# A latent-attention layer with a block-quantised FFN: the weight quantisation moved into the weight-transpose stage, and four tile buffers for the two x sweeps

## The chip, the cores and the metric

The kernel runs on the 8 cores of one Trainium2 chip. Each core works alone on its part, without collectives: core pairs share one of the four batch rows, and each core of a pair owns every other block of 128 tokens. The metric is device time in microseconds (us) of the slowest core. The time before is 4926.94 us, the median of 2 runs (4926.56 to 4927.32).

## The reference

```python
xn = _layernorm(x, axis=-1)                       # x: (4, 4096, 1024) f32
x = x + attn(xn, Wq, Wkv, Wk, Wv, Wo, q_g, k_g) + ffn(xn, weight, bias)

def attn(x, ...):                                 # 16 heads of 64
    q  = rms_norm((x @ Wq) per head, q_g)         # only the first 32 of 64 are used in scores
    kv = x @ Wkv                                  # 128 latent columns
    k  = rms_norm((kv @ Wk) per head, k_g)        # 32 per head
    v  = (kv @ Wv) per head                       # 32 per head
    probs = softmax(causal(q[..., :32] @ k.T / 8))
    return pad(probs @ v) @ Wo

def ffn(x, weight, bias):                         # blocks of 32 along the row
    def quant(t): s = max(max|block| / 7.5, 1e-30); return nearest_on_fp6_grid(block / s) * s
    return quant(x) @ quant(weight).T + bias
```

## The kernel before

Every engine runs one hand-written program. The same Python walk is emitted once for each engine, and `Walk._emit` turns each operation's list of tokens into semaphore waits on the engine that runs it; DMAs are issued by SyncE ("sync") in program order, so a DMA that waits holds every DMA behind it. A transpose (`pet`, L156) and most matmuls (`mm`, L151) wait for `w.tok("dv")`, which is the last VectorE operation emitted so far. All DMA issues have the line L144, and the waits before them L108.

The stages follow each other:

- **Statistics** (`stats`, L387 on). 32 tiles of 128 tokens of x are loaded, alternating between the two halves of `o_tm` (`tmt(0)`, `tmt(1)`). VectorE forms the row sum (L395), the square into `qs(3)` (L397) and its row sum (L400). A tile buffer is free when L400 is done. `stat_finish` turns the sums into mean and reciprocal deviation.
- **kv** (L481 to L517). The 32 tiles are loaded again into the same two buffers. Each is transposed in eight pieces, with a copy out of PSUM after each (L504), and multiplied by Wkv; the buffer is free after the last product (L512).
- **q** (L591 to L664). The same over the 16 tiles of the core's own tokens: row vectors of mean and deviation (L597, L601, L605), eight transposes and copies (L612), 144 matmuls with Wq (L630 reads them out), the norm (L634 to L657). After tiles 0, 2, 4 ... 14 the function `wd_quant` is called for one of eight tiles of the FFN weight: SyncE loads 128 rows of `dfw` into `xet(0)` or `xet(1)` (the two halves of `o_probs`), VectorE quantises them with `quant` (L332 to L385, 25 operations, result in `qtm()`), and SyncE stores the result to a scratch tensor `dwdq` in DRAM.
- **Weight transposes** (L675 to L689). The eight tiles of `dwdq` are loaded into `tmt`, transposed in eight pieces, and copied to `wdT` (L686).
- **FFN** (to L797). `qtile` loads a tile of x, quantises it (`quant` with mean and deviation, from L329), transposes it and copies it (L756); `ffn_half` multiplies by `wdT`.
- **Attention** in four passes over 1024 keys each, and then **normalisation and output** (L1007 to L1074).

The weight quantisation's order around a q tile is

```python
t_qz = quant(w, o_probs + 1024 * bi2, None, None,
             [t_lw] + ([wdq_st[wt - 1]] if wt else []))
wdq_st[wt] = dma("sync", dwdq[128 * wt:128 * wt + 128, :], qtm()[:], waits=[t_qz])
```

Of the kernel before, what the change touches and what calls it, by code (L numbers as in the profile page):

```python
# [5 lines left out]
F32 = mybir.dt.float32  # L6
OP = mybir.AluOpType
AF = mybir.ActivationFunctionType
AX = mybir.AxisListType.X
# [83 lines left out]
class Walk:  # L93
# [44 lines left out]
    def dma(self, q, out, in_, waits=()):  # L138
        pool = DMA_POOL[q]
        sem = pool[self.rr[q] % len(pool)]  # L140
        self.rr[q] += 1
        prior = self.cnt[sem]
        flow = [(sem, prior)] if prior > 0 else []
        return self._emit(q, lambda e: e.dma_start(out=out, in_=in_), sem, 16,  # L144
                          list(waits) + flow)
# [13 lines left out]
    def dve(self, fn, waits=()):  # L159
        return self._emit("vector", fn, "dv", 1, waits)  # L160
# [6 lines left out]
def build_nc(T=4096, stop_after=None):  # L167
# [6 lines left out]
    NO = OWN // 128  # L174

    nc = bass.Bass("TRN2", target_bir_lowering=False)
    dx = nc.dram_tensor("xb", [T, 1024], F32, kind="ExternalInput").ap()
# [8 lines left out]
    dfw = nc.dram_tensor("fw", [1024, 1024], F32, kind="ExternalInput").ap()  # L186
# [7 lines left out]
    dpn = nc.dram_tensor("patnorm", [8, 16, 128], F32, kind="ExternalInput").ap()  # L194
    ddeni = nc.dram_tensor("denind", [1, 528], F32, kind="ExternalInput").ap()
    dout = nc.dram_tensor("out", [1024, OWN], F32, kind="ExternalOutput").ap()
    dwdq = nc.dram_tensor("wdq", [1024, 1024], F32, kind="Internal").ap()

    from contextlib import ExitStack
    es = ExitStack()  # L200
    with es:
# [17 lines left out]
        o_probs = alloc(2 * 1024)  # L219
# [13 lines left out]
        o_tm = alloc(2 * 1024)  # L233
# [26 lines left out]
        idt = lambda: tl(o_id, 128)  # L260
        rowp = lambda p0, off, w: tl(o_rows + off, w, p0, 1)
        stc = lambda k, c, w=1: tl(o_stat + k * 32 + c, w)
# [4 lines left out]
        tmt = lambda i: tl(o_tm + i * 1024, 1024)  # L267
        qs = lambda i, off=0, w=1024, p0=0, p=128: tl(o_qs + i * 1024 + off, w, p0, p)
        qsc = lambda i: tl(o_qsc + i * 32, 32)
        qtm = lambda: tl(o_qtm, 1024)  # L270
# [9 lines left out]
        xet = lambda i: tl(o_probs + 1024 * i, 1024)  # L280
# [106 lines left out]

        def stats(w, dsrc, ntiles, tuse):
            dve, dma = w.dve, w.dma
            last = None  # L390
            for it in range(ntiles):
                bi = it % 2
                t_l = dma("sync", tmt(bi)[:], dsrc[128 * it:128 * it + 128, :],
                          waits=[tuse[bi]])
                t1 = dve(lambda e, it=it, bi=bi: e.reduce_sum(  # L395
                    stc(0, it), tmt(bi)[:], AX), waits=[t_l])
                t2 = dve(lambda e, bi=bi: e.tensor_tensor(qs(3), tmt(bi)[:],  # L397
                                                          tmt(bi)[:], OP.mult),
                         waits=[t1])
                last = dve(lambda e, it=it: e.tensor_reduce(  # L400
                    stc(1, it), qs(3), AX, OP.add), waits=[t2])
                tuse[bi] = last
            return last

        def stat_finish(w, n, t_in):
# [16 lines left out]
        def emit(w: Walk):  # L422
            dve, act, mm, pet, dma = w.dve, w.act, w.mm, w.pet, w.dma
# [17 lines left out]
            for i in range(8):  # L441
# [9 lines left out]
                waits=[t_eps])  # L451
# [8 lines left out]
                    waits=[t])  # L460
            for rr in range(4):
# [3 lines left out]
                     waits=[t, t_o16])  # L465
# [5 lines left out]
            for i in range(8):  # L471
# [3 lines left out]
                         waits=[tmm])  # L475

            tuse = [None, None]
            t_st = stats(w, dx, NT, tuse)
            t_fin = stat_finish(w, NT, t_st)

            tuse = [t_fin, t_fin]  # L481
            t_kv_prev = None
            for it in range(NT):
                bi = it % 2
                t_l = dma("sync", tmt(bi)[:], dx[128 * it:128 * it + 128, :],
                          waits=[tuse[bi]])
                tpm = pet(bank(3, 0, 128, 0, 1), stc(0, it), idt(),
                          waits=[t_fin, w.tok("dv")])
                t_evm = dve(lambda e: e.tensor_copy(mrow(), bank(3, 0, 128, 0, 1)),
                            waits=[tpm])  # L490
                tpa = pet(bank(6, 0, 128, 0, 1), stc(3, it), idt(),
                          waits=[t_fin, w.tok("dv")])
                t_eva = dve(lambda e: e.tensor_copy(arow(), bank(6, 0, 128, 0, 1)),
                            waits=[tpa])
                tra = mm(bank(7, 0, 128), onesr(128), arow(), True, True,
                         waits=[t_eva, t_or])
                t_ar = dve(lambda e: e.tensor_copy(areps(), bank(7, 0, 128)),
                           waits=[tra])
                t_ev = []
                for ci in range(8):  # L500
                    tp = pet(bank(ci // 4, 128 * (ci % 4), 128),
                             tmt(bi)[:, 128 * ci:128 * ci + 128], idt(),
                             waits=[t_l, w.tok("dv")])
                    t_ev.append(dve(lambda e, ci=ci: e.tensor_copy(  # L504
                        xfms(ci), bank(ci // 4, 128 * (ci % 4), 128)), waits=[tp]))
                for ci in range(8):
                    tmm = mm(bank(2, 0, 128), wkvt(ci), xfms(ci), ci == 0, False,
                             waits=[t_ev[ci]] + ([t_kv_prev] if ci == 0 else []),
                             inc=False)
                tmm = mm(bank(2, 0, 128), cskv(), mrow(), False, True,  # L510
                         waits=[t_evm, t_cskv])
                t_kv = dve(lambda e, it=it: e.tensor_tensor(  # L512
                    kvf(128, 128 * it), bank(2, 0, 128),
                    areps()[0:LAT, :], OP.mult), waits=[tmm, t_ar])
                t_kv_prev = t_kv
                tuse[bi] = t_kv
            t_kv_done = w.tok("dv")  # L517

            if stop_after == "A":
                tA = dma("sync", dout[0:LAT, 0:min(OWN, T)], kvf(min(OWN, T), 0),  # L520
                         waits=[t_kv_done])
# [3 lines left out]
            t_wq = []  # L525
            for i in range(8):
                t_wq.append(dma("sync", wqt(i), dwq[128 * i:128 * i + 128, :],
                                waits=[t_kv_done]))
            tuse = [t_kv_done, t_kv_done]
            tg1 = pet(bank(4, 0, 128, 0, NT), stc(2, 0, NT), idt(),  # L530
                      waits=[t_fin, w.tok("dv")])
            tg1e = dve(lambda e: e.tensor_copy(tl(o_scr2, 128, 0, NT),
                                               bank(4, 0, 128, 0, NT)),
                       waits=[tg1])
            tg2 = pet(bank(5, 0, 128, 0, NT), stc(3, 0, NT), idt(),
                      waits=[t_fin, w.tok("dv")])
            tg2e = dve(lambda e: e.tensor_copy(tl(o_scr2 + 128, 128, 0, NT),
                                               bank(5, 0, 128, 0, NT)),
                       waits=[tg2])
            g1 = mm(bank(4, 128, 128, 0, NO), oselt(), tl(o_scr2, 128, 0, NT),  # L540
                    True, True, waits=[tg1e, t_osel])
            g2 = mm(bank(5, 128, 128, 0, NO), oselt(),
                    tl(o_scr2 + 128, 128, 0, NT), True, True,
                    waits=[tg2e, t_osel])
            e1 = dve(lambda e: e.tensor_copy(tl(o_scr2, 128, 0, NO),
                                             bank(4, 128, 128, 0, NO)),
                     waits=[g1])
            e2 = dve(lambda e: e.tensor_copy(tl(o_scr2 + 128, 128, 0, NO),
                                             bank(5, 128, 128, 0, NO)),
                     waits=[g2])  # L550
# [5 lines left out]
                     waits=[b1])  # L556
            f2 = dve(lambda e: e.tensor_copy(stc(3, 0, NO), bank(5, 256, NO)),
                     waits=[b2])
            t_fin = dve(lambda e: e.tensor_scalar(stc(0, 0, NO), stc(2, 0, NO),
                                                  -1.0, None, OP.mult),  # L560
                        waits=[f1, f2])
            t_csq = None
            for ch in range(2):
                for i in range(8):
# [3 lines left out]
                             inc=i == 7)  # L568
                t_csq = dve(lambda e, ch=ch: e.tensor_copy(
                    csq(512 * ch, 512), bank(7, 0, 512, 0, 1)), waits=[tmm])  # L570
            t_pe0 = w.tok("pe")
            wdq_st = [None] * 8
            t_wdq_use = [None, None]

            def wd_quant(wt):
                bi2 = wt % 2
                t_lw = dma("sync", xet(bi2)[:],
                           dfw[128 * wt:128 * wt + 128, :],
                           waits=[t_pe0, t_kv_done] +
                                 ([t_wdq_use[bi2]] if t_wdq_use[bi2] else []))  # L580
                t_qz = quant(w, o_probs + 1024 * bi2, None, None,
                             [t_lw] + ([wdq_st[wt - 1]] if wt else []))
                wdq_st[wt] = dma("sync", dwdq[128 * wt:128 * wt + 128, :],
                                 qtm()[:], waits=[t_qz])
                t_wdq_use[bi2] = t_qz

            t_prev_q = [None] * 8
            t_prev_rep = None
            t_prev_lnq = None
# [1 line left out]
            for ot in range(NO):  # L591
                bi = ot % 2
                t_l = dma("sync", tmt(bi)[:], dxo[128 * ot:128 * ot + 128, :],
                          waits=[tuse[bi]])
# [64 lines left out]
                        scr2(256, 128), OP.mult), waits=[t_rp])  # L659
                    t_prev_rep = t_32  # L660
                tuse[bi] = t_32
                for wt in range(8):
                    if wt * NO // 8 == ot:
                        wd_quant(wt)  # L664
            t_q32_done = w.tok("dv")

            if stop_after == "B":
# [7 lines left out]
            t_wdT = None  # L675
            for wt in range(8):
                bi = wt % 2
                t_l = dma("sync", tmt(bi)[:], dwdq[128 * wt:128 * wt + 128, :],
                          waits=[tuse[bi], wdq_st[wt], t_wq[wt]])
                tp_last = None  # L680
                for ci in range(8):
                    tp = pet(bank(ci // 4, 128 * (ci % 4), 128),
                             tmt(bi)[:, 128 * ci:128 * ci + 128], idt(),
                             waits=[t_l, w.tok("dv")])
                    tp_last = tp
                    t_wdT = dve(lambda e, ci=ci, wt=wt: e.tensor_copy(  # L686
                        wdT(ci)[:, 128 * wt:128 * wt + 128],
                        bank(ci // 4, 128 * (ci % 4), 128)), waits=[tp])
                tuse[bi] = tp_last  # L689
            if stop_after == "C0":  # L690
                for ci in range(4):
                    dma("sync", dout[128 * ci:128 * ci + 128, 0:min(OWN, 1024)],
# [438 lines left out]
```

How the kernel before makes its waits and increments, by code:

```python
    def wait(self, engname, tok):  # L103
        if tok is None or self.cur != engname:
            return
        sem, val = tok
        if val > self.waited[sem]:
            self.h.wait_ge(self.sems[sem], val)
            self.waited[sem] = val
# [16 lines left out]
    def _emit(self, engname, fn, inc, amt, waits):  # L126
        for t in waits:
            self.wait(engname, t)
        if self.cur == engname:
            inst = fn(self.h)
            if inc is not None and inst is not None:
                inst.then_inc(self.sems[inc], amt)
        if inc is not None:
            self.cnt[inc] += amt
            return (inc, self.cnt[inc])
        return None
```

## Time and profile before

| | us |
|---|---|
| median of 2 runs | 4926.94 |
| the profiled execution | 4966.13 |
| span of its slowest core (core 3) | 4964.5 |
| spans of all cores | 4917.7 to 4964.5 |
| TensorE (PE) busy | 3414.2 (69%) |
| VectorE (DVE) busy | 1221.0 (25%) |
| ScalarE (ACT) busy | 627.3 (13%) |

The profile is one execution, read on its slowest core. Busy shares are averages over stages that differ: the page's slices show VectorE at 7 tenths in the first and around 1600 to 2000 us, and TensorE near 9 tenths only in attention. "PE" is a matmul or transpose, "PEld" the load of its stationary operand, "SPq" SyncE's queue, and the granted clock (PEclk) is the share of full speed that TensorE was given, so 0.50 is 1.2 GHz and 1.00 is 2.4 GHz. A wait "A <- B" is idle time of A that ended when B was done.

### The profile page before, as it was taken

Reading aid. Unit: us, or ns where it says so; the run is one execution under the profiler, and the core shown is the slowest. Engines: PE = TensorE matmul, PEld = TensorE weight load, DVE = VectorE, ACT = ScalarE, POOL = GpSimd, SP = SyncE. Lnnn points to the kernel's source line nnn. Section 1 sums busy time; section 2 is a strip of 40 time slices with the busy share of each in tenths; the row PEclk is TensorE's granted clock in tenths of the full one; section 3 lists DMA queues with packets and bytes.
Section 4 is the critical chain, followed back from the end, with each engine's and each line's share of the span. In section 5 each row is a group of like instructions: output and inputs, shape, how many; then the busy total and the mean of one; then the engine's idle time right before and its main releaser. Section 6 shows DMA issues by size and latency. Waiting matters only on the chain.

```text
span 4964.5 us, 61945 instructions; the slowest of 8 cores (4917.7 to 4964.5 us)
## 1 busy us (share of the span) xinstructions
PE 3414.2 (69%) x26106; PEld 2629.1 (53%) x26106; DVE 1221.0 (25%) x2264; ACT 627.3 (13%) x587; POOL 85.2 (2%) x164
## 2 busy tenths in 40 slices
PE   0455555555554146547899999799987997955787
PEld 0233334444443012212588888388874883755777
DVE  7322223333333666671100000200001002022000
ACT  0000000000000000000133433034330331210000
POOL 0000000000000000000000000000000000001111
PEclk6555566766666567768699999699986997866787
DMA  3111010000000100000000000000000000000221
GB/s 121 59 34 39 30 60 17 17 17 17 18 17 26 34 13 30 34 17 26 1 2 2 2 2 2 0 2 2 2 1 1 2 2 1 18 22 22 61 64 56
DMA packets 53208, 110.38 MB, mean 22 GB/s; under 512 B 8838, under 2 KB 27078, under 8 KB 52936
## 3 DMA queue, kind: packets, MB, share of 16 engines
q1 hardware_dynamic: 47816, 97.89, 6.1%
q0 software_dynamic: 5120, 8.53, 0.7%
q8 instruction: 211, 3.46, 0.3%
q14 instruction: 61, 0.50, 0.0%
HBM read 85.29 MB, written 20.97 MB: 21 GB/s over the span
## 4 chain that ended last, share of the span: by engine, by line
PE 61%; DVE 20%; issue 7%; ACT 7%; DMA 4%; SPq 1%; DVEq 1%; POOL 0%; ACTq 0%; POOLq 0%
PE psA L151 35%; PE psB L151 20%; ACT arena L935 6%; PE psA L156 5%; DMA arena<-xown 2%; DVE arena L504 1%; SPq L144 1%; DVE arena L397 1%; DVE arena L395 1%; DVE arena L756 1%; DVEq L108 1%; DVE arena L612 1%; DVE arena L400 1%; DMA arena<-arena 1%; DVE arena L879 1%
## 5 line engine op out<-in xcount | busy, mean ns | idle before, releaser
L151 PE MATMUL psA<-arena 32*128 32x128 f32 (+5 forms) x15616 | 2081.5, 316 | 336.2 <-DVE arena L1007 103.3
L151 PEld LDWEIGHTS psA<-arena 32*128 32x128 f32 (+4 forms) x15616 | 1783.1, 210 | 640.4 <-issue 608.9
L151 PE MATMUL psB<-arena 128*64 128x128 f32 (+3 forms) x9814 | 1078.7, 327 | 241.8 <-ACT arena L935 74.5
L151 PEld LDWEIGHTS psB<-arena 128*64 128x64 f32 (+3 forms) x9814 | 741.2, 155 | 547.9 <-issue 528.7
L935 ACT ACTIVATE arena<-psA,arena 128x1024 f32<-128x1024 f32 x544 | 604.2, 1115 | 1334.5 <-PE psA L151 1334.5
L156 PE MATMUL psA<-arena 128*128 128x128 f32 (+1 forms) x608 | 263.2, 433 | 729.4 <-DVE arena L385 255.4
L156 PEld LDWEIGHTS psA<-arena 128*128 128x128 f32 (+1 forms) x608 | 106.5, 175 | 886.6 <-issue 886.6
L967 DVE TENSOR_TENSOR arena<-psB,arena 128x1024 f32<-128x1024 f32 x24 | 29.4, 1225 | 936.6 <-PE psB L151 936.6
L156 PE MATMUL psB<-arena 128*1 128x128 f32 (+2 forms) x68 | 22.2, 329 | 238.2 <-DVE arena L385 202.4
L642 ACT ACTIVATE arena<-psB,arena 16x128 f32<-16x128 f32 x16 | 5.8, 360 | 1411.4 <-PE psB L151 1411.4
L963 DVE COPY arena<-psB 128x1024 f32<-128x1024 f32 x16 | 19.6, 1225 | 653.9 <-PE psB L151 653.9
L156 PEld LDWEIGHTS psB<-arena 128*1 128x1 f32 (+2 forms) x68 | 5.5, 83 | 255.6 <-issue 255.6
L1074 DVE TENSOR_TENSOR arena<-psA,arena 128x128 f32<-128x128 f32 x128 | 28.4, 283 | 379.0 <-PE psA L151 378.8
L504 DVE COPY arena<-psA 128x128 f32<-128x128 f32 x256 | 74.7, 292 | 181.3 <-PE psA L156 181.3
L841 ACT ACTIVATE arena<-psA,arena 16x1024 f32<-16x1024 f32 x4 | 4.4, 1107 | 859.8 <-PE psA L151 859.8
L630 DVE TENSOR_TENSOR arena<-psA,arena 128x128 f32<-128x128 f32 x128 | 28.3, 284 | 327.8 <-PE psA L151 327.8
L144 POOL DMA_DIRECT2D arena<-arena x32 | 16.6, 524 | 4527.9 <-DVE arena L967 4389.3
L144 POOL DMA_DIRECT2D arena<-out x128 | 68.4, 535 | 322.4 <-DVE arena L1074 302.5
L879 DVE COPY arena<-psA 128x512 f32<-128x512 f32 x64 | 27.7, 433 | 181.3 <-PE psA L151 181.3
L612 DVE COPY arena<-psA 128x128 f32<-128x128 f32 x128 | 37.3, 292 | 106.0 <-PE psA L156 106.0
L756 DVE COPY arena<-psA 128x128 f32<-128x128 f32 x128 | 37.3, 292 | 102.2 <-PE psA L156 102.2
L655 DVE COPY arena<-psB 128x128 f32<-128x128 f32 x64 | 18.7, 292 | 125.1 <-PE psB L151 125.1
(84 smaller groups left out, 937.4 us busy)
## 6 DMA issues: line engine op xcount, KB each, us to landing
arena<-xb SPq DMA_DIRECT2D x64, 512.0 KB, 3.5
arena<-xown SPq DMA_DIRECT2D x48, 512.0 KB, 4.4
out<-arena SPq DMA_DIRECT2D x32, 256.0 KB, 2.1
arena<-out POOLq DMA_DIRECT2D x128, 64.0 KB, 2.5
out<-arena SPq DMA_DIRECT2D x128, 64.0 KB, 2.0
arena<-wq SPq DMA_DIRECT2D x8, 512.0 KB, 9.5
arena<-fw SPq DMA_DIRECT2D x8, 512.0 KB, 5.7
wdq<-arena SPq DMA_DIRECT2D x8, 512.0 KB, 3.0
```

Of the source, the lines that this page charges most:

```text
L108: self.h.wait_ge(self.sems[sem], val)
L144: return self._emit(q, lambda e: e.dma_start(out=out, in_=in_), sem, 16, list(waits) + flow)
L151: lambda e: e.matmul(out, lhsT, rhs, start=start, stop=stop, tile_position=tp, skip_group_check=skipg),
L156: return self._emit("tensor", lambda e: e.transpose(out, in_, ident), "pe", 1, waits)
L395: t1 = dve(lambda e, it=it, bi=bi: e.reduce_sum(stc(0, it), tmt(bi)[:], AX), waits=[t_l])
L397: t2 = dve(lambda e, bi=bi: e.tensor_tensor(qs(3), tmt(bi)[:], tmt(bi)[:], OP.mult), waits=[t1])
L400: last = dve(lambda e, it=it: e.tensor_reduce(stc(1, it), qs(3), AX, OP.add), waits=[t2])
L504: t_ev.append(dve(lambda e, ci=ci: e.tensor_copy(xfms(ci), bank(ci // 4, 128 * (ci % 4), 128)), waits=[tp]))
L612: t_ev.append(dve(lambda e, ci=ci: e.tensor_copy(xfms(ci), bank(ci // 4, 128 * (ci % 4), 128)), waits=[tp]))
L756: e.tensor_copy(xdfm2(par, ci, 128 * sub, 128), bank(ci // 4, 128 * (ci % 4), 128)), waits=[tp])
L879: t_v = dve(lambda e, tc=tc, c0=c0, cw=cw, bk=bk: e.tensor_copy(vaug(tc, c0, cw), bank(bk, 0, cw)), waits=[tmm])
L935: te = act(lambda e, hf=hf, par=par: e.activation(pb(par, hf), ps[:, 1024 * hf:1024 * hf + 1024], AF.Exp, bias=zcol(), scale=1.0), waits=[ ...
```

## The change

Three things are done. In `stats` and in the kv loop the x tiles rotate over four buffers instead of two, the two of `o_tm` and the two of `o_probs`; in `stats` a buffer counts as free after the square (L397) and no longer after the second sum (L400). `wd_quant` is deleted, with its calls between the q tiles, its loads, its stores and the scratch tensor. In the weight stage each tile is loaded from `dfw` itself, quantised there, and transposed from `qtm()`.

```diff
         def stats(w, dsrc, ntiles, tuse):
+            bufs = [tmt(0), tmt(1), xet(0), xet(1)]
+            tuse4 = [tuse[0], tuse[1], tuse[0], tuse[1]]
             for it in range(ntiles):
-                bi = it % 2
-                t_l = dma("sync", tmt(bi)[:], dsrc[128 * it:128 * it + 128, :],
-                          waits=[tuse[bi]])
+                bi = it % 4
+                t_l = dma("sync", bufs[bi][:], dsrc[128 * it:128 * it + 128, :],
+                          waits=[tuse4[bi]])
...
-                tuse[bi] = last
+                tuse4[bi] = t2
...
-            tuse = [t_fin, t_fin]
+            abufs = [tmt(0), tmt(1), xet(0), xet(1)]
+            tuse4 = [t_fin] * 4
             for it in range(NT):
-                bi = it % 2
-                t_l = dma("sync", tmt(bi)[:], dx[128 * it:128 * it + 128, :],
-                          waits=[tuse[bi]])
+                bi = it % 4
+                t_l = dma("sync", abufs[bi][:], dx[128 * it:128 * it + 128, :],
+                          waits=[tuse4[bi]])
...
-                tuse[bi] = t_kv
+                tuse4[bi] = t_kv
...
-            def wd_quant(wt):
-                bi2 = wt % 2
-                t_lw = dma("sync", xet(bi2)[:],
-                           dfw[128 * wt:128 * wt + 128, :],
-                           waits=[t_pe0, t_kv_done] +
-                                 ([t_wdq_use[bi2]] if t_wdq_use[bi2] else []))
-                t_qz = quant(w, o_probs + 1024 * bi2, None, None,
-                             [t_lw] + ([wdq_st[wt - 1]] if wt else []))
-                wdq_st[wt] = dma("sync", dwdq[128 * wt:128 * wt + 128, :],
-                                 qtm()[:], waits=[t_qz])
-                t_wdq_use[bi2] = t_qz
...
-                for wt in range(8):
-                    if wt * NO // 8 == ot:
-                        wd_quant(wt)
...
             for wt in range(8):
                 bi = wt % 2
-                t_l = dma("sync", tmt(bi)[:], dwdq[128 * wt:128 * wt + 128, :],
-                          waits=[tuse[bi], wdq_st[wt], t_wq[wt]])
-                tp_last = None
+                t_l = dma("sync", tmt(bi)[:], dfw[128 * wt:128 * wt + 128, :],
+                          waits=[tuse[bi]] + ([t_wq[wt]] if True else []))
+                t_qz = quant(w, o_tm + bi * 1024, None, None, [t_l])
                 for ci in range(8):
                     tp = pet(bank(ci // 4, 128 * (ci % 4), 128),
-                             tmt(bi)[:, 128 * ci:128 * ci + 128], idt(),
-                             waits=[t_l, w.tok("dv")])
-                    tp_last = tp
+                             qtm()[:, 128 * ci:128 * ci + 128], idt(),
+                             waits=[t_qz, w.tok("dv")])
...
-                tuse[bi] = tp_last
+                tuse[bi] = t_qz
```

## Rows read from the trace of the kernel before

**Rows 1.** Stretches, core 3: length, PE, PEld, DVE, ACT, POOL busy, PEclk, DMA share, GB/s
```profile
16.60:154.00 137.40, 3.81 (x18) 1.97 (x18) 118.52 (x118) 1.93 (x3) 0.00 (x0) 0.55 0.41 127
...
651.00:1585.00 934.00, 518.45 (x2880) 408.93 (x2879) 310.24 (x648) 12.16 (x32) 0.00 (x0) 0.68 0.05 18
1585.00:1652.00 67.00, 28.52 (x64) 11.67 (x64) 18.38 (x63) 0.00 (x0) 0.00 (x0) 0.50 0.21 71
...
2314.00:4388.00 2074.00, 1848.53 (x18877) 1508.92 (x18876) 153.92 (x167) 613.25 (x552) 0.00 (x0) 0.86 0.01 2
```

**Rows 2.** Waits of the q stage, 650 to 1585 (total us, times, longest us)
```profile
PE psB L156 <- DVE arena L385: 202.4, 8, 25.6
...
PE psA L156 <- DMA arena<-xown: 20.5, 8, 3.1
...
PE psB L156 <- DVE arena L657: 6.6, 7, 0.9
PE psA L156 <- DVE arena L605: 4.3, 8, 0.5
```

**Rows 3.** Timeline behind one weight quantisation (start, duration, [idle before <- releaser])
```profile
1419.93 0.33 SPq L144 DMA_DIRECT2D wdq<-arena  x1
1419.94 0.37 PE L156 MATMUL psB<-arena 128*1 128x128 f32 x1 [25.21 <-DVE arena L385]
1420.38 1.19 SPq L144 DMA_DIRECT2D arena<-xown  x2
...
1425.63 0.45 PE L156 MATMUL psA<-arena 128*128 128x128 f32 x1 [3.13 <-DMA arena<-xown]
```

**Rows 4.** Stretches: transposes after a quantisation, after a tile, and a quantisation
```profile
1420.00:1432.80 12.80, 4.80 (x12) 2.12 (x12) 2.89 (x10) 0.00 (x0) 0.00 (x0) 0.50 0.47 164
...
1469.00:1478.90 9.90, 4.51 (x11) 1.87 (x11) 2.89 (x10) 0.00 (x0) 0.00 (x0) 0.50 0.00 0
...
1394.30:1419.90 25.60, 0.43 (x2) 0.13 (x1) 22.34 (x27) 0.00 (x0) 0.00 (x0) 0.50 0.00 0
```

**Rows 5.** L151 psA, core 3: eight stretches behind a quantisation (sum), seven others
```profile
sum 200.30, PE 179.78; mean PE 22.47
...
1243.40:1271.00 27.60, 25.12 (x145) 0.76 0.00 1
...
1478.50:1502.00 23.50, 20.64 (x145) 0.93 0.00 1
sum 168.90, PE 150.94; mean PE 21.56
```

**Rows 6.** The same two sums on core 7
```profile
sum 188.60, PE 168.51; mean PE 21.06
...
sum 164.50, PE 147.31; mean PE 21.04
```

**Rows 7.** Timeline at the weight stage's start, and behind the first x quantisation
```profile
1584.99 51.71 SPq L144 DMA_DIRECT2D arena<-wdq  x8
...
1588.86 0.45 PE L156 MATMUL psA<-arena 128*128 128x128 f32 x1 [4.79 <-DMA arena<-wdq]
...
1677.69 0.45 PE L156 MATMUL psA<-arena 128*128 128x128 f32 x1 [25.63 <-DVE arena L385]
```

**Rows 8.** Statistics lines of VectorE (count, busy us, mean ns, idle before and releaser)
```profile
L400 DVE TENSOR_REDUCE arena<-arena 128x1 f32<-128x1024 f32 x32 | 39.0, 1220 | 3.3
L395 DVE TENSOR_REDUCE arena<-arena 128x1 f32<-128x1024 f32 x32 | 38.8, 1214 | 0.5 <-DMA arena<-xb 0.4
```

**Rows 9.** Waits of the kv stage, 154 to 623
```profile
PE psA L156 <- DMA arena<-xb: 2.2, 1, 2.2
```

**Rows 10.** DMA issues of the q stage (count, size of one, median us to landing)
```profile
arena<-fw SPq DMA_DIRECT2D x8, 512.0 KB, 5.7
```

**Rows 11.** The output stage by stretch, core 3 and core 4
```profile
4563.80:4960.70 396.90, 319.35 (x2231) 313.74 (x2230) 28.13 (x128) 0.00 (x0) 64.13 (x120) 0.78 0.21 61
...
4556.50:4924.70 368.20, 287.94 (x2232) 282.90 (x2230) 28.17 (x128) 0.00 (x0) 64.45 (x120) 0.89 0.23 66
```

More of the change, by code:

```diff
@@ L196, in build_nc @@
     dout = nc.dram_tensor("out", [1024, OWN], F32, kind="ExternalOutput").ap()
-    dwdq = nc.dram_tensor("wdq", [1024, 1024], F32, kind="Internal").ap()
     from contextlib import ExitStack
@@ L389, in stats @@
             dve, dma = w.dve, w.dma
+            bufs = [tmt(0), tmt(1), xet(0), xet(1)]
+            tuse4 = [tuse[0], tuse[1], tuse[0], tuse[1]]
             last = None
             for it in range(ntiles):
-                bi = it % 2
-                t_l = dma("sync", tmt(bi)[:], dsrc[128 * it:128 * it + 128, :],
-                          waits=[tuse[bi]])
+                bi = it % 4
+                t_l = dma("sync", bufs[bi][:], dsrc[128 * it:128 * it + 128, :],
+                          waits=[tuse4[bi]])
                 t1 = dve(lambda e, it=it, bi=bi: e.reduce_sum(
-                    stc(0, it), tmt(bi)[:], AX), waits=[t_l])
-                t2 = dve(lambda e, bi=bi: e.tensor_tensor(qs(3), tmt(bi)[:],
-                                                          tmt(bi)[:], OP.mult),
+                    stc(0, it), bufs[bi][:], AX), waits=[t_l])
+                t2 = dve(lambda e, bi=bi: e.tensor_tensor(qs(3), bufs[bi][:],
+                                                          bufs[bi][:], OP.mult),
                          waits=[t1])
@@ L501, in emit @@
                     tp = pet(bank(ci // 4, 128 * (ci % 4), 128),
-                             tmt(bi)[:, 128 * ci:128 * ci + 128], idt(),
+                             abufs[bi][:, 128 * ci:128 * ci + 128], idt(),
                              waits=[t_l, w.tok("dv")])
@@ L570, in emit @@
                     csq(512 * ch, 512), bank(7, 0, 512, 0, 1)), waits=[tmm])
-            t_pe0 = w.tok("pe")
-            wdq_st = [None] * 8
-            t_wdq_use = [None, None]
-            def wd_quant(wt):
-                bi2 = wt % 2
-                t_lw = dma("sync", xet(bi2)[:],
-                           dfw[128 * wt:128 * wt + 128, :],
-                           waits=[t_pe0, t_kv_done] +
-                                 ([t_wdq_use[bi2]] if t_wdq_use[bi2] else []))
-                t_qz = quant(w, o_probs + 1024 * bi2, None, None,
-                             [t_lw] + ([wdq_st[wt - 1]] if wt else []))
-                wdq_st[wt] = dma("sync", dwdq[128 * wt:128 * wt + 128, :],
-                                 qtm()[:], waits=[t_qz])
-                t_wdq_use[bi2] = t_qz
             t_prev_q = [None] * 8
@@ L677, in emit @@
                 bi = wt % 2
-                t_l = dma("sync", tmt(bi)[:], dwdq[128 * wt:128 * wt + 128, :],
-                          waits=[tuse[bi], wdq_st[wt], t_wq[wt]])
-                tp_last = None
+                t_l = dma("sync", tmt(bi)[:], dfw[128 * wt:128 * wt + 128, :],
+                          waits=[tuse[bi]] + ([t_wq[wt]] if True else []))
+                t_qz = quant(w, o_tm + bi * 1024, None, None, [t_l])
                 for ci in range(8):
                     tp = pet(bank(ci // 4, 128 * (ci % 4), 128),
-                             tmt(bi)[:, 128 * ci:128 * ci + 128], idt(),
-                             waits=[t_l, w.tok("dv")])
-                    tp_last = tp
+                             qtm()[:, 128 * ci:128 * ci + 128], idt(),
+                             waits=[t_qz, w.tok("dv")])
                     t_wdT = dve(lambda e, ci=ci, wt=wt: e.tensor_copy(
```

## The prediction

> **What bounds the kernel now.** I read the busy time by stage first [rows 1]. Core 3, the slowest of the profiled execution, spends 2074 of its 4964.5 us in attention (2314 to 4388), and no edit touches that stage. The edits lie in four earlier stretches: the row statistics (16.6 to 154 us), the kv projection (154 to 623), the q projection with the weight quantisation between its tiles (651 to 1585), and the weight transposes (1585 to 1652). What is to be seen in each row is which engine is full. In the statistics VectorE is busy 118.52 of 137.40 us and DMA only 0.41 of its time. In the q stage and the weight stage no engine is full (in the former TensorE 518 and VectorE 310 of 934 us): they are chains of waits between engines, so only what sits in that chain counts.
>
> The second view is the table of waits of the q stage [rows 2]. TensorE waits 202.4 us, eight times, for the last line of the weight quantisation (L385), and 20.5 us, eight times, for the load of the next x tile. The third is the order of events at one such place [rows 3]. SyncE is held in front of the store of the quantised weight until VectorE has finished; the store leaves at 1419.93, and the x loads behind it leave only at 1420.38. TensorE, released at 1419.94, does its three small operations and then stands 3.13 us until x has landed. So the late x load is a consequence of where the store stands in SyncE's queue.
>
> **The statistics: four buffers, released one operation earlier.** The stage would gain if VectorE waited for loads. It does not: its first operation on a tile waited 0.5 us in all over 32 tiles, 0.4 of it for x, while its two sums take 1.21 and 1.22 us a tile, and neither shows another releaser [rows 8]. Gain 0.4 us, and no more than 0.5.
>
> **The kv stage: four buffers.** The only wait for x in it is the first, 2.2 us [rows 9]; it follows the token of the finished statistics, which the change keeps, so two more buffers can't shorten it. Four loads instead of two leave at that point; if the first came later by their company, the price would be at most the difference of two landings seen, 5.7 us (the weight loads of the q stage, which follow other loads) [rows 10] against 3.9 us (a first load, 1584.99 to 1588.86) [rows 7], so 0 to +1.8 us. I take 0, since 3.9 us is the row of a first load with another right behind it, which is the nearer case.
>
> **The q stage: the weight quantisation leaves.** Eight loads, eight quantisations and eight stores go. Was the quantisation hidden? During one of them TensorE is busy 0.43 us in 25.6 (the last of [rows 4]), and it waits 202.4 / 8 = 25.30 us there against 6.6 / 7 = 0.94 us at a tile boundary without one [rows 2]. So each stands on the path with 24.36 us, and the eight with 194.9 us. Nothing covered them; they are removed here and come back below.
>
> What really goes is the hold in SyncE's queue. Without the store, the x load of the next tile waits only for its own buffer, free since the tile before last, so it leaves a whole tile earlier, some 49 us (from 1420 to the next tile's transposes at 1469 [rows 4]), against a flight of 5.25 us (1420.38 to 1425.63 [rows 3]). The 20.5 us of waits become ordinary waits for the copy of L605, which take 4.3 us over eight tiles [rows 2]. Gain 20.5 - 4.3 = 16.2 us. Bounds: 20.5 us at most, and 0 if the load were late for another reason.
>
> The stretch of 144 matmuls in each tile is a smaller term. On core 3 it takes 22.47 us on average in the eight tiles behind a quantisation and 21.56 us in seven others [rows 5], 0.91 us apart, so 8 x 0.91 = 7.3 us if all tiles become like the others. One of the seven is an outlier of 25.12 us at a granted clock of 0.76, a mean between the levels of 1.2 and 2.4 GHz; without it the others average (150.94 - 25.12) / 6 = 20.97 and the gain would be 12.0 us. On core 7 the two kinds take 21.06 and 21.04 us [rows 6], a gain of 0.2 us. I take 7 us, core 3's own figure with all its rows, and keep 0 to 12.
>
> Why so little, although TensorE idles 25 us? Because it is at the lower level anyway when a tile begins: granted clock 0.50 (1.2 GHz) both in the transposes behind a quantisation and in those behind another tile (the first two of [rows 4]). The Trainium skill (TensorE: Matmul & The Clock Gate, section "Why this matters for your kernels") says that an idle gap between bursts of matmuls sends the clock back to half, and asks to avoid such gaps. By it alone one would promise each of the eight stretches a warm start; the trace agrees that the clock is low after the gap, but not that the gap makes it low, since the chain of small transposes does so too.
>
> **The weight transposes: the quantisation arrives.** Each of the eight weight tiles now runs load, quantisation, then eight pairs of transpose and copy, and all three share VectorE or wait for it, so nothing overlaps. The instructions are those of the q stage on the same shapes, so 8 x 24.36 = 194.9 us come back: net 0. The nearest other row is the quantisation of the x tile that follows: TensorE waits 25.63 us for it [rows 7] against 4.3 / 8 = 0.54 us where a pair follows a pair [rows 2], 25.09 us, with one small operation and two scalings more than the weight form has. By that row it would be 200.7 us, +5.8 us. Bounds -1 to +6; I take 0.
>
> The first load of this stage was exposed for 4.79 us [rows 7] and stays so: same size, same token, from the weight itself instead of the scratch copy. Its landing lies between 3.9 and 5.7 us [rows 7, 10], so 0 to +1.8 us; I take 0. Later loads have 24 us of quantisation in front of them. What SyncE issues next, the first x load of the FFN, waits for a buffer that is now free after the quantisation, not after the last transpose: earlier than before, and it was hidden already. The scratch's eight stores and eight loads vanish from SyncE; nothing else queued on it in these stages.
>
> **Sum.** -0.4 (statistics) + 0 (kv) - 16.2 (x loads) - 7 (stretches) + 0 (moved quantisation) + 0 (first weight load) = -24 us of core 3's 4964.5 us, in an execution of 4966.13 us. This execution is 39 us above the median of 4926.94. Much of that is the output stage, which on core 3 takes 396.9 us at a clock of 0.78 and on core 4 368.2 us at 0.89 [rows 11], 28.7 us that core 4 did not need. The saving is in stages that all cores have alike, so I take it from the median: 4926.94 - 24 = 4903 us. Term by term the ends are: best -0.5 - 20.5 - 12 - 1 = -34, worst +1.8 - 0 - 0 + 6 + 1.8 = +10 us.
>
> **Rivals.**
> - *The moved work was free, or becomes free.* If the quantisation were hidden in the weight stage, 194.9 us would go: 4903 - 195 = 4708 us. Against it: the stage has 18 us of VectorE and 29 us of TensorE work in 67 us [rows 1], nothing to hide 195 us under, and the copies stand behind the next quantisation on the same engine. The mirror image, that it was free before, would add 195 us: 5098 us; TensorE's 0.43 us of 25.6 [rows 4] speaks against it. 2 in 100 each.
> - *The x load stays late* (the change doesn't do what it says): something else, such as four cores of a die reading at once, holds it. Then the 16.2 us stay, and with the ends of the other small terms the time is 4913 to 4937 us; with their taken values it is 4919. For it: the flight itself is 5.25 us, not only the issue. Against it: the issue at 1420.38 directly behind the store [rows 3]. 14 in 100.
> - *The stretches warm up for good.* With no long idle between tiles all sixteen would shed part of their slow beginning, and a stretch would fall to the best seen, 20.64 us (clock 0.93), from core 3's mean of (179.78 + 150.94) / 15 = 22.05 us [rows 5]: 16 x 1.41 = 22.6 us instead of 7, so about 4887 us. The Trainium skill's rule on idle gaps, from the page named above, points this way. Against it: 0.50 in the transposes of either kind of tile [rows 4]. 8 in 100.
> - *The other side: dense stretches closer together lower the clock.* Without the idle fifth of the stage (195 of 934 us) all cores run their 144 matmuls with less pause. If every stretch became like the one of 25.12 us at 0.76, the price would be 16 x (25.12 - 22.05) = 49 us, less 16.6 us gained: about 4960 us, slower than before. It decides from about six such stretches on (6 x 3.07 = 18 us). For it: that row stands in a tile directly behind another. Against it: six of the seven such tiles are the fast ones. 8 in 100.
>
> **How the numbers follow.** The forecast (between -34 and -12 us, so 4893 to 4915) has 66 in 100, the late load 14, warm stretches 8, low clock 8, the two ends of the moved work 2 each. The range is 4885 to 4930: it takes in the warm case and most of the late load, and leaves out the low clock and the two ends. Two per cent of the time, 99 us, is about what a measurement of this kernel can tell from no change; only the moved work being free, now or before, passes it. So faster 0.02, same 0.96, slower 0.02.
>
> **What the profile after would show.** The TensorE waits for x in the q stage fall from eight to none; that stage shrinks from 934 us to about 934 - 195 - 23 = 716; the weight stage grows from 67 to about 262 us; L385 is again waited for, now by the transposes of the weights, with some 25 us each; statistics and kv stage stay within 2 us. Wrong would be: a weight stage under 200 us or above 275, x waits left in the q stage, stretches of 25 us in most tiles, or an attention stage that moves by more than the terms above.

## The result and the profile after

The changed kernel takes 0.9938 of the time of the kernel before, with a 95% interval of 0.9918 to 0.9959: 0.9938 x 4926.94 = 4896 us (4887 to 4907), where 4903 was forecast. In some executions of every kernel here the cores of one die run some per cent longer at a lower granted clock, so ratios leave those out, and the medians over all 36 and 35 executions, 5028.78 and 4968.68 us, say nothing of the change. The lowest execution took 4900.6 us after and 4926.56 before, 26.0 us less.

The stretches of core 3 after, to set against [rows 1] (the columns are those of that group):

```profile
16.60:153.00 136.40, 4.08 (x18) 1.98 (x18) 117.78 (x117) 1.84 (x3) 0.00 (x0) 1.00 0.42 128
...
650.00:1361.00 711.00, 505.49 (x2880) 396.89 (x2880) 136.21 (x448) 12.18 (x32) 0.00 (x0) 0.74 0.03 11
1361.00:1624.00 263.00, 28.52 (x64) 11.62 (x64) 193.77 (x266) 0.00 (x0) 0.00 (x0) 0.50 0.06 20
2276.00:4354.00 2078.00, 1846.38 (x18880) 1505.05 (x18880) 155.82 (x177) 613.24 (x552) 0.03 (x1) 0.86 0.01 2
```

The q stage went from 934 to 711 us and the weight stage from 67 to 263. TensorE's work in the q stage is the same 2880 operations; what left is VectorE's 174 us of busy time (310.24 - 136.21), which now stands in the weight stage (193.77 against 18.38). The windows of the other two stages shown differ from those before by 1 us (statistics) and 4 us (attention).

The waits of TensorE in the q stage after (core 3; total us, times, longest), to set against [rows 2]:

```profile
PE psB L156 <- DVE arena L643: 14.1, 15, 0.9
PE psA L156 <- DVE arena L591: 8.7, 16, 0.5
```

The waits of the weight stage after, core 3:

```profile
PE psA L156 <- DVE arena L384: 204.0, 8, 29.2
...
DVE arena L331 <- DMA arena<-fw: 3.6, 1, 3.6
```

In the q stage all 15 tile boundaries are now ordinary ones of 0.94 us, and no wait for x is left: the copy before the first transpose (L591) releases all 16 tiles. The quantisation is waited for eight times in the weight stage, 204.0 / 8 = 25.5 us each on average; the longest, 29.2, holds the exposed first load of 3.6 us.

The stages of all eight cores of the two profiled executions, from the last VectorE operation of one stage to the last of the next, in us:

| core | q before | q after | weight before | weight after | both, difference |
|---|---|---|---|---|---|
| 0 | 963.9 | 710.9 | 67.1 | 262.9 | -57.2 |
| 1 | 950.5 | 710.4 | 67.1 | 262.6 | -44.6 |
| 2 | 925.1 | 711.0 | 67.2 | 262.9 | -18.4 |
| 3 | 934.6 | 710.8 | 67.6 | 262.6 | -28.8 |
| 4 | 933.2 | 710.8 | 67.5 | 262.6 | -27.3 |
| 5 | 928.3 | 711.5 | 67.1 | 264.0 | -19.9 |
| 6 | 929.8 | 710.0 | 67.2 | 263.2 | -23.8 |
| 7 | 929.9 | 711.3 | 67.4 | 262.5 | -23.5 |

The weight stage takes the same on every core within 0.5 us before and 1.5 us after. The q stage was spread over 39 us before and over 1.5 us after. Most of the 39 us is not the change's doing: on cores 0 and 1 the granted clock stood at 0.81 for a part of the 144 matmuls in 9 and 10 of the 16 q tiles, while on the other six cores it went from 0.50 to 1.00 in every tile and never stood at 0.81. These are a stretch of core 0 with 0.81 and one of core 3 without (columns as in [rows 1]):

```profile
976.00:988.00 12.00, 12.00 (x53) 11.10 (x52) 0.29 (x1) 0.00 (x0) 0.00 (x0) 0.50 0.01 1
989.00:1002.00 13.00, 13.00 (x86) 11.86 (x86) 0.89 (x4) 0.00 (x0) 0.00 (x0) 0.81 0.00 0
...
1244.30:1256.00 11.70, 11.70 (x51) 10.80 (x50) 0.29 (x1) 0.00 (x0) 0.00 (x0) 0.50 0.01 1
1257.00:1269.00 12.00, 12.00 (x91) 10.77 (x90) 0.88 (x4) 0.00 (x0) 0.00 (x0) 1.00 0.00 1
```

On cores 2 to 7 the spread before was 9.5 us, from 925.1 to 934.6. That this fell to 1.5 us was not forecast, and the experiments had to explain it.

### The profile page after: what moved, and what is told of

Read it like the earlier page. It is cut to its first block, busy times and chain, and to the rows that moved or that the text cites. A ratio compares the mean times of both kernels' runs of the same rounds, so it can differ in the third digit from the quotient of the medians.

```text
span 4920.9 us, 61898 instructions; the slowest of 8 cores (4890.0 to 4920.9 us)
## 1 busy us (share of the span) xinstructions
PE 3378.3 (69%) x26106; PEld 2590.4 (53%) x26106; DVE 1221.0 (25%) x2264; ACT 627.3 (13%) x587; POOL 85.2 (2%) x164
## 4 chain that ended last, share of the span: by engine, by line
PE 60%; DVE 20%; issue 8%; ACT 7%; DMA 3%; SPq 1%; DVEq 1%; POOL 0%; ACTq 0%; POOLq 0%
PE psA L151 35%; PE psB L151 19%; ACT arena L917 6%; PE psA L156 6%; DMA arena<-xown 2%; DVE arena L506 1%; SPq L144 1%; DVE arena L398 1%; DVE arena L396 1%; DVEq L108 1%; DVE arena L738 1%; DVE arena L598 1%; DMA arena<-arena 1%; DVE arena L861 1%; DVE arena L373 1%
## 5 line engine op out<-in xcount | busy, mean ns | idle before, releaser
L151 PE MATMUL psA<-arena 32*128 32x128 f32 (+5 forms) x15616 | 2026.7, 311 | 340.1 <-DVE arena L989 102.4
L151 PEld LDWEIGHTS psA<-arena 32*128 32x128 f32 (+4 forms) x15616 | 1732.8, 205 | 640.5 <-issue 607.2
L151 PE MATMUL psB<-arena 128*64 128x128 f32 (+3 forms) x9814 | 1096.7, 330 | 243.3 <-ACT arena L917 75.6
L151 PEld LDWEIGHTS psB<-arena 128*64 128x64 f32 (+3 forms) x9814 | 752.6, 157 | 554.8 <-issue 537.2
L506 DVE COPY arena<-psA 128x128 f32<-128x128 f32 x256 | 74.7, 292 | 180.8 <-PE psA L156 180.8
L144 POOL DMA_DIRECT2D arena<-out x128 | 68.4, 535 | 295.0 <-DVE arena L1056 276.0
L738 DVE COPY arena<-psA 128x128 f32<-128x128 f32 x128 | 37.4, 292 | 108.5 <-PE psA L156 108.5
L598 DVE COPY arena<-psA 128x128 f32<-128x128 f32 x128 | 37.4, 292 | 90.2 <-PE psA L156 90.2
L1001 DVE COPY arena<-psA 128x128 f32<-128x128 f32 x128 | 28.3, 284 | 49.8 <-PE psA L151 49.8
```

The lines of the kernel that those rows point to most:

```text
L151: lambda e: e.matmul(out, lhsT, rhs, start=start, stop=stop, tile_position=tp, skip_group_check=skipg),
L506: t_ev.append(dve(lambda e, ci=ci: e.tensor_copy(xfms(ci), bank(ci // 4, 128 * (ci % 4), 128)), waits=[tp]))
L598: t_ev.append(dve(lambda e, ci=ci: e.tensor_copy(xfms(ci), bank(ci // 4, 128 * (ci % 4), 128)), waits=[tp]))
L738: e.tensor_copy(xdfm2(par, ci, 128 * sub, 128), bank(ci // 4, 128 * (ci % 4), 128)), waits=[tp])
```

## The experiments

Three questions were open. Is the gain really the held x load, or something that went with the quantisation? What are the four buffers worth? And why do the 144-matmul stretches come out nearly all alike? Two theories stood for the last. By the first, the 25 us of idle in front of every second tile made its stretch slow, so that removing the idle time healed it. By the second, idling had nothing to do with it: a stretch's length depends on when it begins against the steps of the clock (the moments at which the granted clock rises from 0.50), and the late loads scattered those beginnings.

### The x load ahead of the weight's load and store, nothing else

```diff
                 tuse[bi] = t_32
+                if ot + 1 < NO:
+                    nb = (ot + 1) % 2
+                    t_lx = dma("sync", tmt(nb)[:],
+                               dxo[128 * ot + 128:128 * ot + 256, :],
+                               waits=[tuse[nb]])
                 for wt in range(8):
                     if wt * NO // 8 == ot:
                         wd_quant(wt)
```

(the load at the head of the tile becomes `t_l = t_lx`)

> The quantisation stays between the q tiles; only the load of the next x tile is issued ahead of the weight's load and store. Theory (the waiting store holds the x load in SyncE's queue): no TensorE wait for x is left in the q stage, and the stage of a core that was at 930 us falls by 16 to 23 us to about 910; the whole by about 18 us (ratio 0.996). Rival (the load is late for another reason, its flight or contention): eight waits of 2 to 3 us stay, the stage stays at 930 and the ratio at 1.000. On the stretches of 144 matmuls: if idling behind a quantisation makes them longer, the eight behind one stay about 0.9 us longer on average than the others; if it does not, the two kinds are alike within 0.3 us.

The ratio was 0.9956 (0.9912 to 0.9999). The q stage of the four cores whose granted clock never stood at 0.81 in a stretch (0, 1, 6 and 7) took 902.3, 903.2, 902.3 and 899.6 us, some 27 us under the 930 of before and so more than the 16 to 23 us expected from the waits. On the other four the clock stood at 0.81 in 14 to 16 of the 16 stretches, and the stage took 944.0 to 952.3 us. On core 0 these are the waits of TensorE in the q stage, the two longest:

```profile
PE psB L156 <- DVE arena L385: 202.4, 8, 25.6
PE psA L156 <- DVE arena L613: 61.3, 112, 0.9
```

The quantisation is waited for exactly as before, 202.4 us in eight waits [rows 2], and the waits for x are gone. So it was the store in SyncE's queue that held the x load; the rival of a load that is late by itself falls.

The stretches answer the other question. This is core 0's chain of work that ended last, q tiles 1 to 8 (start, us); tiles 1, 3, 5 and 7 stand behind a quantisation:

```profile
727.67 20.08 PE psA L151 x144
771.47 20.35 PE psA L151 x144
839.73 20.36 PE psA L151 x144
883.33 20.69 PE psA L151 x144
951.90 20.59 PE psA L151 x144
996.29 20.58 PE psA L151 x144
1064.96 20.38 PE psA L151 x144
1108.51 20.73 PE psA L151 x144
```

Both kinds are alike, 20.08 to 20.59 us behind a quantisation and 20.35 to 20.73 directly behind another tile, although TensorE still idles 25 us in front of every second one. The first theory falls: idling does not lengthen the stretch. And the q and weight stages together take 902.3 + 67.2 = 969.5 us on core 0, no more than the 973.8 us of the changed kernel. Moving the load by a few lines gains what the whole change gains; the two ratios lie within each other's intervals.

### The quantisation moved, the sweeps with two buffers

The edit is the changed kernel with `stats` and the kv loop as before.

> Only the quantisation is moved; the two x sweeps keep two buffers. Theory (four buffers are worth under 1 us): the same as the changed kernel, q stage 711, weight stage 263 us, statistics 125 instead of 124 us, ratio 0.994. Rival (the four buffers carry part of the gain): ratio at or above 0.997, the kv or the statistics stage longer by 5 us or more than in the changed kernel.

The ratio was 0.9972 (0.9927 to 1.0018), which doesn't tell the two theories apart; the stages do. On core 3 the q stage took 711.0 us, the weight stage 262.9, the statistics 125.9 and the kv stage 467.6 (after: 710.8, 262.6, 124.1, 468.4). All of the gain but 1 to 2 us is there without the four buffers. The evenness is not a property of the changed kernel either: on cores 4 and 5 of this execution the q stage took 749.0 and 754.8 us against 710.2 to 711.5 on the other six, again with 0.81 in 13 of 16 stretches. This is one of core 4:

```profile
855.00:874.00 19.00, 18.77 (x121) 16.69 (x119) 1.01 (x5) 0.00 (x0) 0.00 (x0) 0.81 0.00 1
```

### Four buffers alone

> Only the four buffers of the two x sweeps, with the quantisation left between the q tiles. Theory (VectorE, not loads, sets the statistics): statistics 124.1 instead of 124.8 to 125.9 us, kv stage 466 to 470 us as before, q stage 925 to 935 us on undisturbed cores, whole 4926 us, under 1 us of gain. Rival (they matter): statistics or kv shorter by 5 us or more.

Statistics 124.1 us on all cores but one (124.2), kv stage 466.7 to 470.2 us, q stage 927.8 to 949.3 us (927.8 to 930.6 on the four cores without 0.81 in a stretch), one execution of 4952.45 us. The lines of VectorE in its statistics, to set against [rows 8]:

```profile
L402 DVE TENSOR_REDUCE arena<-arena 128x1 f32<-128x1024 f32 x32 | 39.0, 1219 | 3.3
L397 DVE TENSOR_REDUCE arena<-arena 128x1 f32<-128x1024 f32 x32 | 38.7, 1209 | 0.0
```

The wait of 0.4 us for x is gone, and that was all that these lines waited for loads; the stage as a whole is 0.7 to 1.8 us shorter than before, core by core. TensorE's eight waits for x in the q stage are still there, 23.4 us on core 3.

### The quantisation under the matmuls

If the quantisation costs 195 us wherever it stands alone, it should cost nothing beside the matmuls. VectorE idles twice in each q tile while TensorE works through its 144 matmuls. Here the 25 operations of a weight tile are cut into four pieces and run in those gaps of two q tiles; store and scratch tensor stay, the x load goes out one tile ahead.

```diff
                 t_qe = []
+                wq_piece(ot, 0)
                 for j in range(8):
+                    if j == 4:
+                        wq_piece(ot, 1)
...
-                for wt in range(8):
-                    if wt * NO // 8 == ot:
-                        wd_quant(wt)
```

> The weight quantisation stays in the q stage with its store to the scratch tensor, but is cut into four pieces per weight tile that VectorE runs while TensorE does its 144 matmuls (idle gaps of VectorE of about 10 and 8.6 us in each tile; pieces of 4 to 8 us), and the x load is one tile ahead. Theory (where the quantisation stands alone on the path, it costs 195 us wherever it is put; beside the matmuls it costs nothing): q stage 711 to 720 us, weight stage 67 us, whole about 4710 us, ratio 0.955 to 0.958. Rival (the gaps are not free, because the pieces hold the product's reads or slow the matmuls): q stage 740 us or more, up to 906, ratio 0.965 to 0.996.

The profiled execution, the lowest of four, took 4708.95 us, and its slowest core 4707.4; no ratio was formed for this run. The q stage was 708.7 to 712.0 us over the cores and the weight stage 67.0 to 68.4. The gaps on core 0 (timeline of VectorE; start, us, idle before and releaser):

```profile
935.79 0.69 DVE L364 TENSOR_SCALAR arena<-arena 128x1024 f32<-128x1024 f32 x1
936.59 0.69 DVE L366 TENSOR_SCALAR arena<-arena 128x1024 f32<-128x1024 f32 x1
940.70 0.89 DVE L669 TENSOR_TENSOR arena<-psA,arena 128x128 f32<-128x128 f32 x4 [3.41 <-PE psA L160]
...
944.95 0.69 DVE L373 TENSOR_SCALAR arena<-arena 128x1024 f32<-128x1024 f32 x1
949.91 0.88 DVE L669 TENSOR_TENSOR arena<-psA,arena 128x128 f32<-128x128 f32 x4 [4.26 <-PE psA L160]
```

After the first piece VectorE still waits 3.41 us for the matmuls, and after the second 4.26. Here the pieces do not hold TensorE, and as the q stage is no longer than that of the changed kernel and the weight stage is as before, the whole 195 us are hidden.

### The same, with the scratch's first loads early

The edit adds, after the last two quantisations, the load of the first two scratch tiles into the buffers that have become free (`xet(0)`, `xet(1)`).

> The quantisation cut into VectorE's gaps of the q tiles, as in the run before, and in addition the first two tiles of the scratch tensor are loaded during the last q tiles instead of at the start of the weight stage. Theory (only what stands alone on the path costs): q stage 711 us as before, weight stage 63 us instead of 67 because the exposed first load of 4 to 5 us goes, whole about 4704 us, ratio 0.954 to 0.957. Rival (the pieces beside the matmuls cost once more runs are seen, or the first load was hidden anyway): ratio above 0.96, or weight stage 67 us.

The ratio was 0.9555 (0.9541 to 0.9570), the fastest execution 4708.08 us. The weight stage fell to 63.3 us on six cores and 63.5 on the other two, the q stage of six cores was 709.3 to 711.8 (742.0 and 745.7 on cores 6 and 7, where most stretches show 0.81). This version beats both kernels: the one before by 4.4%, the changed one by an estimated 3.9% (0.9555 / 0.9938 = 0.9615).

### A small delay in each tile of the changed kernel

The last group tests the second theory on the stretches: it makes each tile begin a little later than it does in the changed kernel.

```diff
                 tuse[bi] = t_32
+                for k in range(2):
+                    t_dl = dve(lambda e, k=k: e.tensor_copy(qs(k), qtmp(0, 1024)),
+                               waits=[t_32])
```

> The changed kernel with two extra VectorE copies of 0.69 us at the end of each q tile, 1.6 us on the path of each tile. If tile time is a plain sum, the q stage grows by 15 or 16 x 1.6 = 24 to 26 us, from 711 to 736 us, and the stretches of 144 matmuls stay at 20.55 us. If the equal stretches of the changed kernel (15 within 20.33 to 20.76 us, starts 44.37 us apart) come from the tiles falling into step with the steps of the clock, the delay is partly absorbed or overshot: the stage grows by 10 us or less, or by 40 us or more, and the stretches change their length.

> The changed kernel with one extra VectorE copy (0.69 us, 0.8 on the path) at the end of each q tile; two copies (1.6 us) gave 756 us and stretches of 22.7 us, starts 47.78 us apart. Plain sum: 711 + 13 = 724 us, stretches 20.55 us. Steps (tile starts settle on one of a few spacings, of which 44.37 and 47.78 us have been seen): either near 711 us with spacing 44.37, or near 764 us with spacing 47.78, or a mix of tiles of the two spacings; in no case 16 equal tiles of 45.2 us.

> The changed kernel with four extra copies (3.2 us on the path) at the end of each q tile. Plain sum: 711 + 51 = 762 us, stretches 20.55 us, starts 47.6 us apart. Plain sum on top of two copies: 756 + 26 = 782 us. Steps: starts 47.78 us apart as with two copies although 1.6 us more is on the path, stage near 764 us, and the stretches short again (20.4 to 20.8 us), since the longer part of a stretch would be taken up by the delay.

Each of the three was executed once; no stretch of theirs shows 0.81 on any core. What the copies put on the path is read from TensorE's waits at the tile boundaries on core 3: 26.0, 35.1 and 59.0 us over 15 boundaries with one, two and four copies, against 14.1 without. That is less than the expectations took for two and four copies (1.4 and 3.0 us a tile instead of 1.6 and 3.2).

| core 3 | on the path, sum | q stage | growth |
|---|---|---|---|
| none | 0 | 710.8 | |
| one copy | 11.9 | 739.9 | 29.1 |
| two copies | 21.0 | 759.8 | 49.0 |
| four copies | 44.9 | 760.0 | 49.2 |

A plain sum fails: one copy costs two and a half times what it puts on the path, the second another 20 us, the next two together 0.2. On the other seven cores the first copy costs 26 to 39 us, the second 7 to 16 more, the next two 4 to 12. The stretches show where it goes. First core 3 of the changed kernel, tiles 4 to 6, from the chain of work that ended last (start, us):

```profile
839.04 20.55 PE psA L151 x144
883.41 20.55 PE psA L151 x144
927.78 20.56 PE psA L151 x144
```

The same tiles with one copy:

```profile
843.25 24.68 PE psA L151 x144
890.85 20.06 PE psA L151 x144
935.42 24.68 PE psA L151 x144
```

With two copies:

```profile
852.74 22.67 PE psA L151 x144
900.50 22.68 PE psA L151 x144
948.28 22.68 PE psA L151 x144
```

With four copies:

```profile
849.60 20.26 PE psA L151 x144
896.35 20.71 PE psA L151 x144
943.97 20.79 PE psA L151 x144
```

The same 144 matmuls take 20.06 to 24.68 us. The granted clock of the beginning of a stretch tells why. This is a stretch of the changed kernel on core 3 (columns as in [rows 1]):

```profile
883.40:886.00 2.60, 2.60 (x15) 2.60 (x14) 0.29 (x1) 0.00 (x0) 0.00 (x0) 0.50 0.00 0
886.00:890.00 4.00, 4.00 (x28) 3.47 (x28) 0.00 (x0) 0.00 (x0) 0.00 (x0) 0.93 0.01 4
```

And of the kernel with two copies, core 3:

```profile
948.30:951.00 2.70, 2.70 (x14) 2.70 (x14) 0.29 (x1) 0.00 (x0) 0.00 (x0) 0.50 0.02 6
951.00:955.00 4.00, 4.00 (x18) 3.55 (x17) 0.00 (x0) 0.00 (x0) 0.00 (x0) 0.50 0.00 0
955.00:959.00 4.00, 4.00 (x27) 3.41 (x25) 0.00 (x0) 0.00 (x0) 0.00 (x0) 0.85 0.00 0
```

And of the kernel with one copy, core 3, the stretches of 24.68 and 20.06 us:

```profile
843.20:855.00 11.80, 11.80 (x52) 10.90 (x51) 0.29 (x1) 0.00 (x0) 0.00 (x0) 0.50 0.00 0
855.50:868.00 12.50, 12.42 (x93) 11.02 (x92) 0.98 (x4) 0.00 (x0) 0.00 (x0) 1.00 0.01 2
...
890.80:892.90 2.10, 2.10 (x12) 2.10 (x11) 0.29 (x1) 0.00 (x0) 0.00 (x0) 0.50 0.00 0
893.00:911.00 18.00, 17.90 (x134) 15.89 (x133) 0.88 (x4) 0.00 (x0) 0.00 (x0) 1.00 0.00 1
```

All these stretches begin at 0.50 (1.2 GHz) and end at 1.00 (2.4 GHz). In the changed kernel the step comes about 3 us after the start; with two copies it comes only after more than 6.7 us (the mean of 0.85 in the 4 us that follow puts it near 8); with one copy it comes about 12 and about 2 us after it, in turn. The step does not follow the stretch's start by a fixed time, and the later it comes, the longer the stretch: 20.06, 20.55, 22.68 and 24.68 us in this order. If equal tiles keep their place against the steps, that explains why the stretches repeat: tiles 2 to 9 of the changed kernel on core 3 are all alike and 44.37 us apart, tiles 4 to 6 with two copies 47.8, and with one copy two spacings, 47.60 and 44.57 us, take turns, the mix that was among the outcomes expected. What sets the steps themselves was not measured. The Trainium skill (TensorE: Matmul & The Clock Gate, section "What's actually happening") says that the gate's window runs freely and does not start anew with the kernel, so that the point of the rise depends on where the first matmul lands in it. These runs agree that it moves with the beginning, with 20.06 to 24.68 us for one and the same work. By that section it varies by half a microsecond; here it lay between 2 and 12 us after the start, and the measurement decides.

With four copies I expected spacing 47.78 throughout; it was mixed (46.75 and 47.62 us between the three shown), with short stretches and some of 22.7 us. The direction of the second theory held, the exact spacing did not.

## Why the prediction came out as it did

**The place of the gain: right.** The step that found the x loads behind the waiting store [rows 3] is shown by the run that moved only the load. The 16.2 us of waits on core 3 went as forecast (20.5 + 4.3 before, 8.7 after, 16.1 less), on the path named.

**The moved quantisation: right.** 194.9 us were to leave and come back. The weight stage grew by 262.6 - 67.6 = 195.0 us on core 3, and by 195.1 to 196.9 on the other cores. Neither that it was free before nor that it becomes free was true. The first weight load cost 3.6 us against 4.79, 1.2 us less, just outside its bounds of 0 to +1.8 on the good side.

**The buffers: right in kind.** Statistics -1.0 us on core 3, where 0.5 was the most allowed, and kv -0.8, the latter inside the 2 us over which that stage differs between cores anyway.

**The 144-matmul stretches: too small, and for the wrong reason.** Seven us were taken, from the difference between tiles behind a quantisation and others on core 3 [rows 5]. Measured on core 3, the two stages together gained 28.8 us, of which 16.2 are the loads: 12.6 us are left for the stretches, just over the end of the range of 0 to 12. Read directly, the sixteen stretches of core 3 sum to 346.8 us before and 331.3 after, 15.5 us less; the other 3 us came back elsewhere in the tiles, where these runs were not read. On cores 2 and 4 to 7 the same sums differ by 4.1, 9.7, 4.8, 10.1 and -1.5 us, so no figure of one core stood for all; the 39.2 and 24.7 us of cores 0 and 1 hold the clock of 0.81 as well. The step that failed is the one that read the two kinds of tiles as cause and effect, idle time making a tile slow. What the runs show in its place, where the store no longer holds the load and the idle time stays: both kinds are short, 20.08 to 20.73 us. So the waits for x (on core 3 up to 3.1 us, each a little different) moved the tiles' beginnings against the steps of the clock, for both kinds of tile; that removing them alone shortened the stretches is shown, how each wait shifted each tile was not followed. Without those waits the tiles repeat with nearly the same spacing, and this spacing happens to give short stretches. Core 7, where both kinds were fast [rows 6], was not the lower bound of an effect of idling; that its loads happened to keep step is the likely reading, which no run tests on that core.

**The rival of a lower clock** went the other way: the one stretch of 25 us had been seen in a tile directly behind another [rows 5], and with all tiles so placed there was none after the first tile. Its mean clock of 0.76 was no lowered level either: it stood at 0.50 for some 12 us and then at 1.00 (the rows of core 3 in the section on the result). The rival that stretches warm up for good came near in length, but not in sum and not by its mechanism. Its mark of 20.64 us [rows 5] holds one operation more than the stretch; the chain has that stretch at 20.21 us, and the stretches after are 20.33 to 20.76 on cores 3 and 5 from the second tile on. The sum fell by 15.5 us on core 3 where the rival asked for 22.6, and the run with the idle gaps left in has the same short stretches. **The late load** fell.

**The size as a whole.** -24 us was forecast, and the time by the ratio, 4896 us, lies in the range. The q and weight stages of cores 2 to 7, without 0.81 before and after, gained 18.4 to 28.8 us, 23.6 on average; the lowest executions lie 26.0 us apart; the timed ratio makes 31 us, with an interval of 20 to 40. That the total came near is in part luck: it rests on a stretch term read from one core by a wrong cause, while the stretches of the other five gained from -1.5 to 10.1 us. What the forecast did not weigh is that the time is that of the slowest core. In the profile of before, cores 0 and 1 were up to 39 us behind in the q stage with 0.81 in their stretches, and cores 4 and 5 of the run with the moved quantisation alone were some 40 us behind in the same way, so the change does not heal this. How much of the 31 us comes from such stretches in the timed executions can't be settled, since one execution of each kernel has a trace.

## What to carry to other kernels

A DMA that waits holds every DMA behind it on its queue: a store that waits for a result belongs behind the loads that the next tile needs, and moving the load was worth the whole of this change. Work on an idle engine costs its full length wherever the others wait for it, so moving it from one such place to another gains nothing, while cutting it into the gaps of a stage where another engine is busy hid all of it (195 us, 4.0% of the time before). Before adding buffers, look whether the engine behind them ever waits for a load.

## What the runs showed of the hardware that was not expected

On core 3 a delay of 0.79 us in each of 15 tiles, 11.9 us in sum, cost 29.1 us, and three more copies behind it (33 us more on the path) cost 20.1. The clock's rise came about 2, 3, 8 or 12 us after the start of one and the same stretch of matmuls. In some profiled executions the clock stood at 0.81 in many stretches of two or four of the cores, in the kernel before on cores 0 and 1 while cores 2 and 3 of the same die stood at 1.00 there. In a stage that falls to 1.2 GHz and rises again in every tile, the time of a tile depends on where it begins against the clock's steps, so that a difference of some 20 us in such a stage is no proof of what was changed in it; a second delay, or a series of them as here, tells the two apart.
